# Two transformer layers on one core: setup loads in parts, late weights behind the first shifts, gates on other engines

## What is computed

```python
mod = (silu(c) @ wmod).reshape(1, 6, 1, -1)
sa, ca, ga, sb, cb, gb = (mod[:, i] for i in range(6))
ga = (2 * (ga >= 0) - 1) * maximum(abs(ga), 0.25)
gb = (2 * (gb >= 0) - 1) * maximum(abs(gb), 0.25)
h = layernorm(x) * (1 + ca) + sa
q, k, v = h @ Wq.T + bq, h @ Wk.T + bk, h @ Wv.T + bv    # 16 heads of 8
x = x + ga * ((softmax(q @ k.T / sqrt(8)) @ v) @ Wo.T + bo)
h = layernorm(x) * (1 + cb) + sb
x = x + gb * (shared_ffn(h) + one_of_16_experts(h))
```

## Time and profile before

| | |
|---|---|
| median of 3 runs | 1144.68 us (1144.45 to 1147.16) |
| the profiled execution, its own time | 1150.95 us |
| its span, first to last instruction | 1149.2 us |
| busy: PE, DVE, ACT, POOL | 1027.6, 907.4, 819.5, 151.0 us |
| mean granted clock of PE | 0.953 |

### The profile page before, as it was taken

How to read it: one execution, slowest core, us unless ns; L and a number is a source line. 1 busy time by engine, 2 the same in 40 slices (tenths; PEclk the granted TensorE clock), 3 DMA queues, 4 the chain that set the end, 5 groups by cost and what they waited for, 6 DMA issues and landing times.

```text
span 1149.2 us, 22211 instructions
## 1 busy us (share of the span) xinstructions
PE 1027.6 (89%) x8772; PEld 351.4 (31%) x8772; DVE 907.4 (79%) x1174; ACT 819.5 (71%) x1581; POOL 151.0 (13%) x270
## 2 busy tenths in 40 slices
PE   4558999999999999999998999899978888798987
PEld 1212222222222222222232444343434453333314
DVE  5797999998999989999988777666766558587603
ACT  3105999998999998999986676467743546466775
POOL 2004100003000013000033000411031003000101
PEclk9757999999999999999999999999989999899987
DMA  4650500002000001000003331142003220200000
GB/s 106 122 103 15 139 2 2 2 2 43 2 2 2 2 15 29 2 1 3 2 1 111 113 100 29 29 89 52 2 1 111 67 63 22 46 10 2 10 2 10
DMA packets 47309, 42.07 MB, mean 37 GB/s; under 512 B 6150, under 2 KB 45414, under 8 KB 47206
## 3 DMA queue, kind: packets, MB, share of 16 engines
q1 hardware_dynamic: 44950, 35.27, 13.1%
q0 software_dynamic: 1824, 5.25, 1.6%
q10 hardware_dynamic: 432, 0.13, 0.0%
HBM read 26.83 MB, written 13.30 MB: 35 GB/s over the span
## 4 chain that ended last, share of the span: by engine, by line
PE 64%; DVE 18%; ACT 7%; DMA 4%; issue 3%; SPq 2%; POOL 1%; DVEq 0%; POOLq 0%; ACTq 0%
PE O L897 23%; PE T L868 12%; DVE mx L1204 10%; PE S L827 7%; PE S L834 4%; ACT PT L1435 3%; PE T L877 3%; PE S L1008 2%; PE S L966 1%; PE S L976 1%; PE T L1016 1%; DMA rows_k<-q 1%; PE S L967 1%; PE S L877 1%; PE T L906 1%
## 5 line engine op out<-in xcount | busy, mean ns | idle before, releaser
L1204 DVE TENSOR_REDUCE mx<-S 128x2 f32<-128x1024 f32 (+2 forms) x672 | 757.6, 1181 | 90.0 <-PE S L834 37.6
L1435 ACT ACTIVATE PT<-T 128x512 f32<-128x512 f32 (+2 forms) x1280 | 675.8, 580 | 118.4 <-PE T L868 47.8
L897 PE MATMUL O<-PT,Va 128*9 128x256 f32 (+1 forms) x4040 | 319.0, 388 | 3.3 <-ACT Os L1470 3.3
L827 PE MATMUL S<-Ks,Qs 48*128 48x512 bf16 x1024 | 208.2, 398 | 27.7 <-DVE mx L1204 20.9
L868 PE MATMUL T<-Qs,Ks 51*128 51x512 bf16 x1024 | 202.3, 388 | 16.0 <-ACT PT L1435 7.2
L868 PEld LDWEIGHTS T<-Qs,Ks 51*128 51x128 bf16 x1024 | 55.6, 93 | 227.1 <-issue 132.4
L897 PEld LDWEIGHTS O<-PT,Va 128*9 128x9 f32 x4040 | 60.0, 88 | 207.7 <-issue 198.3
L834 PE MATMUL S<-K,Qs 96*128 96x512 bf16 (+3 forms) x320 | 85.5, 357 | 15.0 <-DMA Qs<-rows_q 4.7
L877 PE MATMUL T<-Qs,K 99*128 99x512 bf16 (+3 forms) x256 | 72.2, 350 | 7.7 <-ACT PT L1435 4.1
L897 PE MATMUL O<-PT,V 128*17 128x512 f32 (+3 forms) x640 | 76.2, 549 | 0.0
L827 PEld LDWEIGHTS S<-Ks,Qs 48*128 48x128 bf16 x1024 | 52.6, 95 | 54.9 <-DVE mx L1204 47.0
(11 more groups left out here) (276 smaller groups left out, 836.1 us busy)
## 6 DMA issues: line engine op xcount, KB each, us to landing
Qs<-in_L_ffn_experts SPq DMA_DIRECT2D x28, 192.0 KB, 2.9
Ks<-in_L_ffn_experts SPq DMA_DIRECT2D x20, 192.0 KB, 2.6
Qs<-rows_q SPq DMA_DIRECT2D x48, 64.0 KB
Vf<-sorted_x SPq DMA_DIRECT2D x12, 256.0 KB, 4.7
sorted_y<-Vf SPq DMA_DIRECT2D x12, 256.0 KB, 2.3
Qs<-rows_q SPq DMA_DIRECT2D x24, 128.0 KB, 4.4
rows_q<-q SPq DMA_DIRECT2D x7, 384.0 KB, 2.6
sorted_x<-XP POOLq DMA_DIRECT2D x1, 1792.0 KB, 10.8
```

The source lines that it names most:

```text
L827: m = e.matmul(two[:, i, :], Qs[r0:r0 + 48, hp, q0:q0 + 128], Ks[r0:r0 + 48, hp, CH * kb:CH * kb + CH], start=True, stop=True, tile_positi ...
L897: m = e.matmul(Ob[32 * g:32 * g + d1, lo:hi], v, PT[(2 * j + g // 2) % 4][:, p0 + lo:p0 + hi], start=(kt == 0 and halves[0] == 0), stop=Tr ...
L1204: e.tensor_reduce(mx[:, u % 2, h0:h0 + 2, kb], two[:, :, 0:n], AX.X, ALU.max).then_inc(free, 1)
L1435: e.activation(PT[(2 * j + pair) % 4][:, CH * i + lo:CH * i + CH], bank[:, lo:CH], ACT.Exp).then_inc(free, 1)
```

## The change

- **Setup by parts.** The loads of the four chunks of keys and of query chunk 0 are cut in two: part 0 has head pairs 0 and 1 (all that unit 0 reads), part 1 the other six. All parts 0 come first; the five parts 1 stand behind the rows of ones on SP (`load_rest`), 36 transfers. Scores and steps of the other quads wait for part 1.
- **Two queues.** Of the part 0 of the queries, six of twelve transfers are issued by ACT, behind a wait for their store.
- **Splits.** Those of key chunks 1 to 3 go from DVE to POOL. On DVE statistics and norms move ahead of the splits of key chunk 0 and query chunk 0. The key projections take T2, O and T2 in place of one bank of S.
- **Values** move from before the first score to behind score tiles 8, 10, 12 and 14 of unit 0.
- **Late weights.** The two condition weights and 16 late weights move behind the first unit's shifts in SP's order.
- **Gates.** ACT takes `gates`, `bias_v` and `rows` out of their banks; POOL makes sign and size in five instructions of 128x512 and one of 128x256, adds the bias row and makes the broadcast. DVE keeps none of it.
- **Steps.** `scaled_weights` moves from step 1 to 3, `scaled_weights2` from 3 to 5, `project_q(1)` from 5 to 18, `late_pool` from 8 to 20, `late_constants` from 12 to 24.

```diff
+PARTS = {("k", c): 2 for c in range(4)} | {("q", 0): 2}
...
-    def load_slabs(keep=0):
-        while len(loads) > keep:
-            P.stage("load", *loads.pop(0))
+    rest = []
+    def load_slabs():
+        while loads:
+            kind, c = loads.pop(0)
+            P.stage("load", kind, c, 0)
+            if (kind, c) in PARTS:
+                rest.append((kind, c))
+    def load_rest():
+        while rest:
+            P.stage("load", *rest.pop(0), 1)
...
-    split("k", 0, "dv")
+    P.stage("stats", 0, 2)
     P.norm(0, 1)
     P.turn_h(0, 1, "T1")
+    P.stage("stats", 0, 3)
+    P.norm(0, 2)
+    split("k", 0, "dv")
     split("q", 0, "dv")
-    load_slabs(1)
-    project("k", 1, "S1b")
-    P.stage("stats", 0, 2)
-    P.norm(0, 2)
     load_slabs()
+    project("k", 1, "T2")
+    split("k", 1, "po")
     P.turn_h(0, 2, "T0")
-    split("k", 1, "dv")
-    project("k", 2, "S1a")
-    P.stage("stats", 0, 3)
     P.norm(0, 3)
     load_slabs()
+    project("k", 2, "O")
+    split("k", 2, "po")
     P.turn_h(0, 3, "T1")
-    split("k", 2, "dv")
-    project("k", 3, "S1b")
     load_slabs()
-    split("k", 3, "dv")
+    project("k", 3, "T2")
+    split("k", 3, "po")
     load_slabs()
     P.stage("constants")
-    for c in range(4):
+    def values(c):
...
-    at(1, scaled_weights)
-    at(3, scaled_weights2)
-    at(5, lambda: project_q(1))
-    at(8, lambda: P.stage("late_pool"))
-    at(12, lambda: P.stage("late_constants"))
+    at(3, scaled_weights)
+    at(5, scaled_weights2)
+    at(18, lambda: project_q(1))
+    at(20, lambda: P.stage("late_pool"))
+    at(24, lambda: P.stage("late_constants"))
...
-    for _ in range(many[0]):
+    for i in range(many[0]):
         emit_s()
+        if i in (7, 9, 11, 13):
+            values((i - 7) // 2)
+        elif i == 15:
+            load_rest()
     for i in range(7):
         if i == 2:
             urgent.pop(0)[1]()
+            P.stage("late_loads")
...
+        def load_q(e, c, par, heads, loaded):
+            cols = slice(CH * c, CH * c + CH)
+            for j, part in enumerate((0, 0, 0, 1, 1, 2)):
+                r0 = 64 * par + 8 * j
+                src = scratch["q"][part, :, cols].rearrange("(d two h) n -> two d h n", two=2, h=8)[par]
+                e.dma_start(Qs[r0:r0 + 8, heads, cols], src[:, heads, :]).then_inc(loaded, 16)
...
+                        pe.wait_ge(rows_loaded["k", kb, int(quad > 0)], LOADED["k"])
+                        pe.wait_ge(rows_loaded["q", c, int(quad > 0 and c == 0)], LOADED["q"])
...
-                elif name == "broadcast":
-                    dv.wait_ge(silu_done, 1)
-                    dv.wait_ge(dv_const, 1)
-                    for l in range(2):
-                        m = e.tensor_scalar(cb[:, l, :], onesf[:, :], cs[:, l:l + 1], None, ALU.mult)
-                    m.then_inc(cb_made, 1)
-                    dv.wait_ge(ld_bv, 16)
-                    e.tensor_scalar(bvb[:, :], onesf[:, :], bv[:, 0:1], None, ALU.mult).then_inc(bv_made, 1)
-                elif name == "gates":
-                    bank, free = filled(("gates",))
-                    dv.tick(e.tensor_scalar(gt[:, 0:CH], bank[:, :], 0.0, 2.0, ALU.is_ge, ALU.mult))
-                    e.tensor_copy(gf, bank[:, :]).then_inc(free, 1)
-                    done(("gates",))
-                    dv.tick(e.scalar_tensor_tensor(gt[:, CH:], gf, -1.0, gf, ALU.mult, ALU.max))
-                    dv.settle()
-                    dv.tick(e.tensor_scalar(gt[:, CH:], gt[:, CH:], 0.25, None, ALU.max))
-                    dv.settle()
-                    dv.tick(e.scalar_tensor_tensor(gf, gt[:, 0:CH], -1.0, gt[:, CH:], ALU.add, ALU.mult))
-                    dv.settle()
-                    e.tensor_scalar(gH[:, :, :], gB[:, 1:4:2, :], 0.5, None, ALU.mult).then_inc(gates_made, 1)
-                elif name == "rows":
-                    bank, free = filled(("rows",))
-                    e.tensor_copy(rows[:, 0, :], bank[:, 0:128])
-                    e.tensor_scalar(rows[:, 1, :], bank[:, 128:256], 1.0, None, ALU.add).then_inc(free, 1)
...
-                elif name == "bias_v":
-                    bank, free = filled(("bias_v",))
-                    e.tensor_tensor(boB[:, :], boB[:, :], bank[:, 0:128], ALU.add).then_inc(free, 1)
...
+                elif name == "load" and tuple(a) == ("q", 0, 0):
+                    ac.wait_ge(rows_stored[P.slot["q", 0]], 16)
+                    load_q(e, 0, 1, slice(0, 2), rows_loaded["q", 0, 0])
...
+                elif name == "gates":
+                    bank, free = filled(("gates",))
+                    e.activation(gf, bank, ACT.Copy).then_inc(free, 1)
+                elif name == "bias_v":
+                    bank, free = filled(("bias_v",))
+                    e.activation(bvb[:, :], bank[:, 0:128], ACT.Copy).then_inc(free, 1)
+                elif name == "rows":
+                    bank, free = filled(("rows",))
+                    e.activation(rows[:, 0, :], bank[:, 0:128], ACT.Copy)
+                    e.activation(rows[:, 1, :], bank[:, 128:256], ACT.Copy, bias=1.0).then_inc(free, 1)
...
+                    done(("gates",))
+                    sign, size = gt[:, 0:CH], gt[:, CH:]
+                    po.tick(e.tensor_scalar(sign, gf, 0.0, 2.0, ALU.is_ge, ALU.mult))
+                    po.settle()
+                    po.tick(e.tensor_scalar(sign, sign, -1.0, None, ALU.add))
+                    po.settle()
+                    po.tick(e.tensor_tensor(size, sign, gf, ALU.mult))
+                    po.settle()
+                    po.tick(e.tensor_scalar(size, size, 0.25, None, ALU.max))
+                    po.settle()
+                    po.tick(e.tensor_tensor(gf, sign, size, ALU.mult))
+                    po.settle()
+                    e.tensor_scalar(gH[:, :, :], gB[:, 1:4:2, :], 0.5, None, ALU.mult).then_inc(gates_made, 1)
...
+                    po.tick(e.tensor_tensor(boB[:, :], boB[:, :], bvb[:, :], ALU.add))
+                    po.settle()
...
-                                e.dma_start(Ks[r0:r0 + 8 * many, :, cols], src).then_inc(loaded, 16)
+                                e.dma_start(Ks[r0:r0 + 8 * many, heads, cols], src[:, heads, :]).then_inc(loaded, 16)
                     elif kind == "q":
                         for par in range(2):
-                            for j, part in enumerate((0, 0, 0, 1, 1, 2)):
-                                r0 = 64 * par + 8 * j
-                                src = scr[part].rearrange("(d two h) n -> two d h n", two=2, h=8)[par]
-                                e.dma_start(Qs[r0:r0 + 8, :, cols], src).then_inc(loaded, 16)
+                            if not (c == 0 and part == 0 and par):
+                                load_q(e, c, par, heads, loaded)
...
+                elif name == "late_loads":
```

More of the change, by code:

```diff
@@ L1751, in sp_program @@
                 elif name == "load":
-                    kind, c = a
+                    kind, c, part = a
                     slot, k, _, _ = split_memory(kind, c)
@@ L1755, in sp_program @@
                     scr = scratch[kind][:, :, cols]
-                    loaded = rows_loaded[kind, c]
+                    loaded = rows_loaded[kind, c, part]
+                    heads = slice(0, 8) if (kind, c) not in PARTS else slice(2, 8) if part else slice(0, 2)
                     sp.wait_ge(rows_stored[slot], 16 * (k + 1))
```

37 lines of the change are left out of this document (22 added, 15 removed).

## The result

**1137.26 us**, the median of four executions (1136.02 to 1138.73), against 1144.59 for the kernel before (four executions, 1144.45 to 1147.16), taken beside it: ratio 0.9931, 95% interval 0.991 to 0.9952, so 7.3 us faster. A second set of runs gave 1134.65 (six) against 1146.89 (eleven): 0.9893, 0.9874 to 0.9913, 12.2 us faster. The forecast was 1137.7, the range 1132 to 1144; both medians lie in it. The profiled execution took 1138.73 us, its span is 1137.0.

What follows compares the result with a forecast made beforehand. PE was taken to hold 64% of the chain that ended last, with four losing stretches in the first 130 us. Terms of -2.8 (first step) and -4.2 (gates) gave -7.0 on 1144.7: 1137.7 us, range 1132 to 1144.

Steps and rivals of the forecast that it cites:

- ACT's hold: Setup: ACT's wait for the query store and its six issues take back some 5 us of what the parts give.
- the sum: Whole kernel: 2.8 us earlier at the first step plus 4.2 at the gates, 7.0 us in all.
- The first score: End of setup on PE: first score at 33.2 us against 36.77, behind the last key projection.
- The values: Unit 0's scores: four value groups at 1.2 GHz each cost DVE 0.95 us, 3.8 together.
- The shifts: Joined maxima to first step: 6.6 us against 8.39 without late weights ahead; first step at 80.5, 2.8 earlier.
- Parts 1: SP's loads before the shifts: the last lands near 79, no wait, but no first step before 79.5.
- Late weights: Behind the shifts on SP: the last lands near 93.5, its reader comes at 97.7; nothing is paid.
- Gates: Unit 0's steps: PE's stop 2.9 us shorter, half-steps at low clock 1.3 less; 4.2 together, bounds 2.5 and 5.
- POOL: Gate chain: three scalar operations at 1.2 us each, chain done at 115.3, before unit 1's shifts near 116; cost 0.
- The rival that the wait goes to POOL: PE's turn of unit 1's shifts waits for POOL's gate chain, up to 5 us: 1142.7, chance 17%.
- Moved only, zero: Second query projection, masks, tables, zero fill and 12 transfers at later steps: zero, within 1 us.

Runs made afterwards that it cites:

- SP alone: Changed kernel with all twelve part-0 query transfers issued by SP, none by ACT: 1142.71 us (0.9897 against the kernel before), in a second timing 1130.54 (0.9873).
- the repeat: The kernel before, unedited, run and profiled once more: 1145.7 us against 1145.4 for itself, ratio 1.0006.
- the combination: Changed kernel with all twelve part-0 query transfers on SP and sixteen single value groups behind score tiles 9 to 24: 1132.11 us, 0.988 against the kernel before.
- the side work in unit 0: Changed kernel with second queries, masks and fill at steps 7, 10 and 14 instead of 18, 20 and 24: 13.1 us lost at unit 2.
- the run with added matmuls: Changed kernel with single value groups plus three unused 128x128 bf16 matmuls behind score tiles from the 17th and unit 1's first seven: unit 0 2.8 us longer than without them.
- the values one by one: Changed kernel with sixteen value groups of two matmuls placed singly behind score tiles 9 to 24, instead of four at a time: single time 1132.84 us.
- the weights ahead: Changed kernel with the 18 late weight transfers back ahead of unit 0's shifts on SP: 8.0 us more from the maxima to the first step.

## Why the prediction was right

The sign held, and so did the chain of causes at four of its steps: ACT's hold, the gaps at value groups, the shifts behind the maxima, the gates. Two terms were too pessimistic (the values, and less so the first score), one belonged to an execution more than to the kernel, and the reason given for a bound (parts 1) did not show. That the median met the forecast within 0.4 us is luck: the head gained 9.9 us where the sum said 7.0, and the stretch behind unit 15, to which the prediction gives no difference, took back 2.6 of it in the first pair of medians and added 2.3 in the second. Point by point, in the steps of the prediction, against the two profiles of each kernel:

- *The first score* at 33.2: measured 31.96 and 31.91. The reading of ACT's order was right, and the run with SP alone shows the cost: forecast "some 5 us", measured 4.6. The missing 1.2 us are many small ones: ACT's wait ended 0.56 earlier (21.34 for 21.9), its six issues took 2.25 for 2.6, and from there to the first score it was 8.37 for 8.7. One reading of the kernel before was wrong: the values were not done by 36 us. The row behind the last one that the earlier trace rows shows of them ends at 36.84 by the model of the profile, so in that profile PE had no idle time before its first score; in the second it waited 0.70 for the query data. Values and data end there at nearly the same time, which is why both had to move: with all else of the change in place, the first score stands at 35.98 with whole loads, at 35.09 with the values first, and at 31.96 with both moved.
- *The values* at 3.8: measured 2.0 and 1.3 (38.77 and 38.07 against 36.74 with none in the stretch). The reason, PE full at the low clock, is right for the groups that left gaps of 0.99 and 0.61. It was mis-sized because the clock did not stay low: it was 0.92 between 46 and 50 us in the first profile, and two groups left no gap; in the second it was 1.00 from 44 to 52 us, and three left none.
- *The shifts*, 6.6 behind the maxima: 6.65 and 6.63. But the gain of 1.8 against 8.39 is the term that failed as a statement on the change. By the repeat the kernel before has 6.65 as well, if its weights' issue is not slowed. The move out of SP's way is worth 0 to 1.7 against the old order. It is needed all the same in the new order: with the parts 1 ahead, weights in the old place cost 8.0 us at the first step.
- *Parts 1* landing "near 79", so that no start before 79.5 was within reach: refuted. The first step was at 77.38 and 76.61, in the runs with SP alone at 72.76 and 72.35. I had scaled the time of whole key chunks; SP issued the 36 transfers in 19.2 us, and no score or step of the changed kernel waits for them. In the combination, whose head is 4.6 us earlier, one score does wait, until 72.42: such a bound exists, but near 72 there.
- *Late weights*: nothing paid, right; the last was issued by 85.38, and the gate groups at 94.20 wait for none.
- *Gates* at 4.2: the run with them on DVE gives 3.9, by 3.0 of stop (2.9 forecast) and 0.9 of clock (1.3). From first step to unit 2 the kernels differ by 4.0 and 4.8 (80.76 and 80.57 against 76.77 and 75.80).
- *POOL*: the scalar operations took 1.94, 1.51 and 1.50, not 1.2, and still less 0.61, near which the cited rule on one input would have put them; the chain ended 1.6 us before its forecast of 115.3 because it began 3.4 earlier (96.08 for 99.5). PE lost 0.5. The rival that the wait goes to POOL did not come true here, but in the run with the side work in unit 0 it does, at 6.66 us.
- *Moved only, zero*: right in its sum, wrong as a reason: in the new order the old places would cost 13.1 us, on POOL and on SP (above).

By the head, the change gains 9.94 us in the first pair of profiles and 9.93 in the second (164.09 to 154.15, 162.34 to 152.41), crosswise 8.2 to 11.7; the sum said 7.0. What was missing in the first pair is 1.2 at the first score and 1.9 between it and the maxima, less 0.2 behind the first step. The medians, 7.3 and 12.2, lie on both sides of the head's gain; what of their difference is the chip and what the execution stays open. The profiles put what differs behind unit 15, in the part that the change doesn't touch.

The version with the ACT transfers back on SP is ahead of the changed kernel in the head, and so of the kernel before: 4.6 and 4.1 us at unit 2, first profiles and second. Its second timing, 1130.54, is the lowest median of the study; there is no direct interval against the changed kernel, and those against the kernel before overlap (the combination, on one chip with the changed kernel, has 1132.11 against 1134.65, with overlapping ranges), so the 4 us are shown at the marks and not by the timings.

## What to carry to other kernels

Moving DMA issues to a second engine is paid at their place in that engine's order: its wait for the data counts for more than the issue. Before an issue goes to ACT or any engine that computes, look at what stands behind it and who waits for that.

A move that is free by itself can be what makes another part possible. Here the side work had to leave unit 0 because the gates went to POOL and unit 1's maxima came earlier than the second queries' transfers allowed, and the late weights had to go behind the shifts because the parts 1 came in front; ask of each moved step what its old place would cost in the new order.

A wait that is read in one profile is one execution's until a second shows it. Where a term of the forecast rests on a slow issue, a second profile tells whether the wait belongs to the kernel.

## What the hardware showed that I had not expected

- **PE full by the profile and still at 0.50.** In the run with added matmuls PE is busy for 4.00 of 4.00 us in windows from 46 to 66 and the granted clock stays 0.50. Behind the first step, in the changed kernel, PE is full too and the clock does rise, to 1.00 by 88 us. Nor does it need added work: with the values one by one PE is busy for 20.00 of 20 us from 40 to 60 at 0.50, while with the same matmuls in groups of four the changed kernel is at 1.00 from 48 to 52. What tells these apart was not settled.
- **A granted clock of 1.00 does not fix a duration.** The two float32 projections of key chunk 1 took 1.10 us in the first profile of the changed kernel (at 16.95) and 2.05 in its second (at 16.92), with 1.00 granted from 17 to 19 in both. In the kernel before, those of chunk 2 took 2.05 at 25.04 with 1.00 granted from 25 to 27, and 2.04 in its second profile with 0.50.
- **The clock's change comes at other times in other executions** of the same order: the first score at 30.9 to 32.1 in seven runs with the same setup (the last key projection took 1.10 us in the three early ones, 2.04 or 2.05 in the four late ones), and 15.5 to 16.9 us from first step to gates in all runs but that with the weights ahead. A single profile can show a gain of 1.7 us at unit 2 that no edit made.
- **An issue has no fixed price.** The same 18 late loads took SP 9.1 us behind the shifts and 13.4 directly behind the parts 1, one of them 2.07 where none took over 1.07. The cause was not isolated.
- **POOL's float32 128x512 operations of one input with scalars** took 1.50 to 1.94 us (like ones on DVE in the kernel before 0.43, and 0.69 out of a bank), longer than its own with two inputs (1.27) and than its copy (0.61).
